# Routing from unscaled rows, zeroing in two parts, and waits between GpSimd's scatters in a gated attention and mixture-of-experts block

## The reference, cut to what matters

```python
# layer 0, attention part: a mixing matrix added to x
x = x + tanh(g_xattn[0]) * L0_xattn(ctx_512, layernorm(x))     # top 76 of 256 per row, sigmoid, symmetrised
# layer 0, feed-forward part: 64 experts, 8 for each token
h = layernorm(x)
logits = h @ gate_w.T                       # (1024, 64)
probs = softmax(logits); topk_w, topk_idx = top_k(probs, 8)
# for each expert e:  out += combine[:, e] * (silu(h @ w13_g.T) * (h @ w13_u.T)) @ w2.T
x = x + tanh(g_ffn[0]) * out
# layer 1: causal attention of 16 heads, and 8 experts plus a shared one
```

## Time and profile before

| | |
|---|---|
| median of 3 runs | 559.7 us (559.28 to 561.05) |
| the profiled execution, its time | 562.27 us |
| the profiled execution, its span in the trace | 560.5 us |
| PE busy | 415.2 us (74%) |
| DVE busy | 342.2 us (61%) |
| ACT busy | 184.9 us (33%) |
| POOL busy | 145.7 us (26%) |
| DMA moved | 82.96 MB |

### The profile page before, as it was taken

One profiled execution on the slowest core, in us unless ns is written; L12 is line 12 of the kernel. 1 busy time (PEld: TensorE's weight loads), 2 busy tenths in 40 slices (PEclk: granted clock), 3 DMA queues, 4 the chain that ended last, 5 costly groups with the idle time before them and its releaser, 6 DMA issues.

```text
span 560.5 us, 9184 instructions
## 1 busy us (share of the span) xinstructions
PE 415.2 (74%) x2710; PEld 351.7 (63%) x2710; DVE 342.2 (61%) x1058; ACT 184.9 (33%) x377; POOL 145.7 (26%) x156
## 2 busy tenths in 40 slices
PE   5344644200999999999616776899789988998796
PEld 3223433200998888998414554787679867996695
DVE  4999793300497448544356784388657885680664
ACT  3122220200333333343271153425363354417321
POOL 4017677575000000000768332411423000000000
PEclk9966565555899999999755679799889999999999
DMA  7999222144999999999422211110111000000000
GB/s 236 427 414 399 83 99 102 61 159 146 278 339 334 325 311 306 350 398 393 142 81 82 60 39 39 47 30 12 58 47 56 2 0 0 20 2 2 2 19 20
DMA packets 36789, 82.96 MB, mean 148 GB/s; under 512 B 6032, under 2 KB 16144, under 8 KB 34960
## 3 DMA queue, kind: packets, MB, share of 16 engines
q1 hardware_dynamic: 23616, 56.48, 29.0%
q0 software_dynamic: 6144, 16.79, 9.2%
q10 hardware_dynamic: 6992, 9.24, 4.6%
HBM read 50.44 MB, written 31.92 MB: 147 GB/s over the span
## 4 chain that ended last, share of the span: by engine, by line
PE 51%; issue 23%; SPq 9%; DVE 7%; ACT 6%; DMA 2%; DVEq 0%; ACTq 0%
PE PS L624 10%; PE PS L634 6%; PE PS L713 5%; PE PS L790 3%; SPq L347 3%; PE PS L687 3%; PE PS L611 3%; PE PS L726 3%; PE PS L728 3%; PE PS L727 3%; PE PS L808 2%; PE PS L775 2%; DMA XE<-slots_in 2%; PE PS L818 2%; SPq L343 2%
## 5 line engine op out<-in xcount | busy, mean ns | idle before, releaser
L467 POOL DMA_INDIRECT GB<-slots_out,IDXG x64 | 69.4, 1084 | 226.5 <-DMA slots_out<-OE 132.3
L624 PE MATMUL PS<-XTE,WR 128*128 128x128 f32 (+2 forms) x512 | 79.6, 299 | 0.0
L460 POOL DMA_INDIRECT slots_in<-XNA,IDX x64 | 62.9, 982 | 33.2 <-issue 18.2
L624 PEld LDWEIGHTS PS<-XTE,WR 128*128 128x128 f32 x512 | 70.3, 193 | 0.4 <-ACT XTE L936 0.2
L1369 DVE TENSOR_TENSOR HE<-SGE,PS 128x128 f32<-128x128 f32 (+2 forms) x64 | 19.9, 311 | 70.1 <-ACT SGE L945 67.2
L634 PE MATMUL PS<-WR,HE 128*80 128x256 f32 (+2 forms) x198 | 53.4, 380 | 0.4 <-issue 0.4
L726 PE MATMUL PS<-XH,WGH 128*128 128x256 f32 x160 | 51.2, 320 | 0.0
L936 ACT COPY XTE<-PS 128x256 f32<-128x256 f32 (+2 forms) x64 | 26.3, 411 | 71.2 <-PE PS L611 71.2
L611 PE MATMUL PS<-CF,XE 80*128 80x80 f32 (+2 forms) x198 | 28.3, 256 | 26.5 <-DMA XE<-slots_in 26.5
L713 PE MATMUL PS<-WD,XW 128*128 128x256 f32 x160 | 42.6, 390 | 5.8 <-DVE TH L1460 5.8
L728 PE MATMUL PS<-XH,WGL 128*128 128x256 f32 x160 | 46.5, 290 | 0.0
(11 more groups left out here) (235 smaller groups left out, 822.2 us busy)
## 6 DMA issues: line engine op xcount, KB each, us to landing
WR<-in_wexp SPq DMA_DIRECT2D x64, 384.0 KB, 5.6
slots_in<-GB SPq DMA_DIRECT2D x12, 1024.0 KB, 19.0
XE<-slots_in SPq DMA_DIRECT2D x24, 160.0 KB, 4.8
slots_out<-OE ACTq DMA_DIRECT2D x24, 160.0 KB
XE<-slots_in SPq DMA_DIRECT2D x29, 128.0 KB, 5.4
slots_out<-OE ACTq DMA_DIRECT2D x24, 128.0 KB
WGU<-in_wgu SPq DMA_DIRECT2D x1, 2560.0 KB
XE<-slots_in SPq DMA_DIRECT2D x11, 192.0 KB, 4.0
```

What stands on the lines that cost most here:

```text
L460: pool.indirect_dma_start(out=xs, out_offset=bass.IndirectOffsetOnAxis(ap=IDX[:, t, j:j + 1], axis=0), in_=XNA[:, t, :], in_offset=None, b ...
L467: pool.indirect_dma_start(out=GB[:, t % BT, j, :], out_offset=None, in_=ys[0:rows, :], in_offset=bass.IndirectOffsetOnAxis(ap=IDXG[:, t, j ...
L624: last = mm(psGE[place % 2][:, a, 0:cap(place)], W13[:, k, a, :], XTE[:, place % 2, k, 0:cap(place)], start=(k == 0), stop=(k == KC - 1))
```

## The change

Five things are different. POOL's `norm_scale` writes to a tile RSN with a column pair for every token tile, so the scale of a batch stays. The gate is made mean-free once (`centre_gate`: PE multiplies the gate by a matrix of -1/256, DVE adds the result), and PE transposes the unscaled rows X1, so that the logits come out as the normalised ones without the factor 1/sqrt(var + eps); the exponential applies this factor (`scale=RSN`), and the emergency path transposes XNA for itself. ACT does the exponential of batch `b` behind `scores(b + 2)` and `base(b + 2)`. Zeroing is in two parts: slots 0 to 127 of every expert (8 DMAs), then slots 128 to 191 (4 DMAs); the first tile's scatters wait for the first part alone. POOL waits, ahead of scatters 10, 11, 13 and 15 of each batch, for the next batch's `summed`, `xn_flipped`, `logits_done` and `ranked`, and `norm_scale` stands ahead of scatter 11 in all batches. DVE's steps stand after other numbers of rounds.

```diff
-ROOT_BEHIND = (None, 10, 7, 7)
+PACE = {10: "summed", 11: "xn_flipped", 13: "logits_done", 15: "ranked"}
+LOW = 128
...
-FIRST_ROUNDS = (1, 3, 5, 6)
-LATER_ROUNDS = (3, 5, 8, 9)
+FIRST_ROUNDS = (1, 2, 2, 3)
+LATER_ROUNDS = (3, 4, 4, 5)
...
             sp.wait_ge(S["zero_set"], 1)
-            for i in range(SLOTS // (8 * P)):
-                sp.dma_start(xs[i * 8 * P:(i + 1) * 8 * P, :].rearrange("(p r) d -> p (r d)", p=P), ZERO)\
-                  .then_inc(S["zeroed"], 16)
+            by_expert = xs.rearrange("(e c) d -> e c d", c=CAP)
+            for e in range(0, E0, 8):
+                part = by_expert[e:e + 8, 0:LOW, :].rearrange("e (q r) d -> q e (r d)", q=16)
+                sp.dma_start(part, ZERO).then_inc(S["zeroed_low"], 16)
+            for e in range(0, E0, 16):
+                part = by_expert[e:e + 16, LOW:, :].rearrange("(x y) (q r) d -> q x y (r d)", y=2, q=16)
+                sp.dma_start(part, ZERO.rearrange("p (y f) -> p y f", y=2)).then_inc(S["zeroed"], 16)
...
+            nc.gpsimd.memset(MINUS_MEAN[:, :], -1.0 / D).then_inc(S["half_set"], 1)
...
-            pool.wait_ge(S["zeroed"], 16 * (SLOTS // (8 * P)))
+            pool.wait_ge(S["zeroed_low"], 16 * (E0 * LOW // (8 * P)))
             for t in range(TT):
+                if t == 1:
+                    pool.wait_ge(S["zeroed"], 16 * (E0 * (CAP - LOW) // (8 * P)))
                 pool.wait_ge(S["xn_ready"], t // BT + 1)
                 pool.wait_ge(S["idx_ready"], t // BT + 1)
                 for j in range(TOP0):
                     b = t // BT + 1
-                    if b < B and t % BT * TOP0 + j == ROOT_BEHIND[b]:
+                    nth = t % BT * TOP0 + j
+                    if b < B and nth in PACE:
+                        pool.wait_ge(S[PACE[nth]], b + 1)
+                    if b < B and nth == 11:
                         norm_scale(b)
...
+            def centre_gate():
+                pe.wait_ge(S["half_set"], 3)
+                for k in range(KC):
+                    last = mm(psN, MINUS_MEAN[:, :], GATE0[:, k, :], start=(k == 0), stop=(k == KC - 1))
+                last.then_inc(S["gate_summed"], 1)
+
             def logits(b):
-                pe.wait_ge(S["xn_ready"], b + 1)
+                pe.wait_ge(S["x1_kept"], b + 1)
                 pe.wait_ge(S["xnt_copied"], b)
                 for k in range(KC):
                     for t in range(BT):
-                        last = nc.tensor.transpose(psX[:, k, t * P:(t + 1) * P], XNA[:, b * BT + t, k * P:(k + 1) * P], ident)
+                        last = nc.tensor.transpose(psX[:, k, t * P:(t + 1) * P], X1[:, b * BT + t, k * P:(k + 1) * P], ident)
...
+                if b == 0:
+                    pe.wait_ge(S["gate_centred"], 1)
...
-                act.wait_ge(S["mask_ready"], b + 1)
-                for t in range(BT):
-                    n = b * BT + t
-                    last = A.activation(C0[:, n, :], psL[:, t, :], ACT.Exp, bias=SM[:, n, 0:1], accum_out=SM[:, n, 1:2])
-                last.then_inc(S["exp_done"], 1)
                 if b + 2 < B:
                     scores(b + 2)
                     base(b + 2)
+                act.wait_ge(S["bias_ready"], b + 1)
+                act.wait_ge(S["rs_ready"], b + 1)
+                for t in range(BT):
+                    n = b * BT + t
+                    last = A.activation(C0[:, n, :], psL[:, t, :], ACT.Exp, scale=RSN[:, n, 0:1], bias=SM[:, n, 0:1], accum_out=SM[:, n, 1:2])
+                last.then_inc(S["exp_done"], 1)
...
-                st.done(V.tensor_scalar(SM[:, b * BT:(b + 1) * BT, 0:1], L8[:, :, 0:1], -1.0, None, ALU.mult))
...
                 V.tensor_tensor(MB[:, b * BT:(b + 1) * BT, :], psL, LR[:, :, :], ALU.not_equal).then_inc(S["mask_ready"], 1)
+                V.scalar_tensor_tensor(SM[:, b * BT:(b + 1) * BT, 0:1], L8[:, :, 0:1], -1.0, RSN[:, b * BT:(b + 1) * BT, 0:1],
+                                       ALU.mult, ALU.mult).then_inc(S["bias_ready"], 1)
+
+            def centre_gate():
+                dve.wait_ge(S["gate_summed"], 1)
+                for k in range(KC):
+                    last = V.tensor_tensor(GATE0[:, k, :], GATE0[:, k, :], psN, ALU.add)
+                last.then_inc(S["gate_centred"], 1)
...
             top_rounds(0, 0, 6)
             base_scale(0, slice(0, BT))
+            centre_gate()
             top_rounds(0, 6, ROUNDS)
```

More of the change, by code:

```diff
@@ L191, in gated_block @@
         LR = sb("LR", [P, BT, E0])
+        RSN = sb("RSN", [P, TT, 2])
+        MINUS_MEAN = sb("MINUS_MEAN", [P, P])
         MB = sb("MB", [P, TT, E0], BF16)
@@ L272, in gated_block @@
             projected qk_copied scores_done sim_copied th_ready masked summed xn_ready xn_flipped
-            xnt_copied logits_done max_ready exp_done dve_scalar dve_mix act_mix x1_kept
+            xnt_copied logits_done exp_done dve_scalar dve_mix act_mix x1_kept
             stats_ready rs_ready coef_ready base_ready var_ready rsx_ready half_set eps_added
             gu_done silu_done h_done o_done o_used
-            zero_set zeroed mask_ready masks_added ranked idx_ready scattered order_set order_done order_ready flag_ready w8_ready
+            zero_set zeroed_low zeroed gate_summed gate_centred bias_ready mask_ready masks_added ranked idx_ready scattered order_set order_done order_ready flag_ready
             all_stored general_done gb_used xt_flipped xt_copied gue_done silue_done he_done oe_done oe_copied dve_w8
@@ L425, in _ @@
             nc.gpsimd.memset(MINUS_HALF[:, :], -0.5).then_inc(S["half_set"], 1)
+            nc.gpsimd.memset(MINUS_MEAN[:, :], -1.0 / D).then_inc(S["half_set"], 1)
             nc.gpsimd.memset(GB[:, 1, 6:, :], 0.0).then_inc(S["half_set"], 1)
-            pool.wait_ge(S["half_set"], 2)
+            pool.wait_ge(S["half_set"], 3)
             def row_scale(part, tiles):
@@ L445, in norm_scale @@
                 pool.wait_ge(S["var_ready"], b + 1)
-                nc.gpsimd.tensor_scalar(RS[:, :, 3:4], MV[:, :, 1:2], EPS, None, ALU.add).then_inc(S["eps_added"], 1)
+                tiles = slice(b * BT, (b + 1) * BT)
+                nc.gpsimd.tensor_scalar(RSN[:, tiles, 1:2], MV[:, :, 1:2], EPS, None, ALU.add).then_inc(S["eps_added"], 1)
                 pool.wait_ge(S["eps_added"], b + 3)
-                nc.gpsimd.tensor_tensor(RS[:, :, 0:1], RS[:, :, 3:4], MINUS_HALF[:, 0:BT].unsqueeze(2), ALU.pow).then_inc(S["rs_ready"], 1)
+                nc.gpsimd.tensor_tensor(RSN[:, tiles, 0:1], RSN[:, tiles, 1:2], MINUS_HALF[:, 0:BT].unsqueeze(2), ALU.pow).then_inc(S["rs_ready"], 1)
             row_scale(1, slice(BT, TT))
             norm_scale(0)
-            pool.wait_ge(S["zeroed"], 16 * (SLOTS // (8 * P)))
+            pool.wait_ge(S["zeroed_low"], 16 * (E0 * LOW // (8 * P)))
             for t in range(TT):
+                if t == 1:
+                    pool.wait_ge(S["zeroed"], 16 * (E0 * (CAP - LOW) // (8 * P)))
                 pool.wait_ge(S["xn_ready"], t // BT + 1)
@@ L649, in all_tokens @@
             def all_tokens():
+                for b in range(B):
+                    pe.wait_ge(S["xnt_copied"], B + b)
+                    for k in range(KC):
+                        for t in range(BT):
+                            last = nc.tensor.transpose(psX[:, k, t * P:(t + 1) * P], XNA[:, b * BT + t, k * P:(k + 1) * P], ident)
+                    last.then_inc(S["xn_flipped"], 1)
+                pe.wait_ge(S["xnt_copied"], 2 * B)
                 with pe.Fori(0, E0 // 2) as i:
@@ L963, in all_tokens @@
                         act.wait_ge(gathered[t][j], 16)
+                for b in range(B):
+                    act.wait_ge(S["xn_flipped"], B + b + 1)
+                    A.copy(XNT[:, :, b * N:(b + 1) * N], psX).then_inc(S["xnt_copied"], 1)
                 with act.Fori(0, E0) as e:
@@ L1180, in mix_norm @@
                 for t in range(BT):
-                    last = V.tensor_scalar(XNA[:, b * BT + t, :], X1[:, b * BT + t, :], MV[:, t, 0:1], RS[:, t, 0:1], ALU.subtract, ALU.mult)
+                    last = V.tensor_scalar(XNA[:, b * BT + t, :], X1[:, b * BT + t, :], MV[:, t, 0:1], RSN[:, b * BT + t, 0:1], ALU.subtract, ALU.mult)
                     if t < BT - 1:
```

## The result

Over 18 runs of each, the changed kernel's median is 556.16 us (551.88 to 558.48) against 559.74 (558.07 to 563.2). The ratio is 0.9941 with a 95% interval of 0.9924 to 0.9958: 3.3 us faster by the ratio (2.4 to 4.3), 3.6 by the medians. The forecast was 9.7, that is 550.0 with an own range up to 552.5; the direction and the path were right, the size was not.

A forecast was written before the change was run, and what follows sets the result against it. POOL's scatter queue was taken to bound the routing stage. Start 6.1 plus waits 5.7 less 0.4 rounding gave 11.4, less 1.7 for late signals 9.7: 559.7 to 550.0 us, own range 547.5 to 552.5, full range 546.5 to 556.5.

The forecast's parts named there:

- the pricing of the late signals: Routing stage, batch 3: engines starting late although their awaited work is done cost 0 to 5.5 us; 1.7 taken.
- clean sum: Routing stage: start 6.1 earlier, waits 5.7 less, minus 0.4 rounding; 11.4 us saved, last scatter ending at 123.6.
- POOL's queue sets the end of the stage and a microsecond off it is one off the time: Routing stage ends with POOL's last scatter, 134.98 before; each microsecond taken from it should come off the time.
- Zeroing in two parts, patterns at full rate: Ahead of the scatters: new patterns cost nothing, low part lands near 32.7, second part is hidden at 43 to 44.
- Mean-free gate, chain of batch 0: Batch 0: two additions cost DVE 0.4 us; slot numbers and first scatter come at 37.0 instead of 43.08.
- Batches 1 to 3 with signals on time: Routing's later batches: POOL waits 1.3 us for batch 1, none for 2 and 3; last scatter ends at 123.6.
- The wait of 4.7 in batch 3 goes: Batch 3: POOL no longer waits for the statistics at scatter 11, where before it lost 4.7 us.
- Rival 1: Batches 2 and 3: late signals return in full, new waits hand them to POOL; saving 5, 554.7 us; chance 0.22.
- Rival 3: Zeroing pattern runs at half rate, low part lands at 54, no scatter before it; 563 us; chance 0.03.
- rival 2: Batches 0 to 2: twelve new waits expose POOL to late signals, costing 14 against 11.4; 562.5 us; chance 0.07.
- Rival 4: Early scatters queue behind second-layer weight loads, the start's 6.1 is lost; 554 to 555 us; chance 0.05.
- the case of no gain: A stage behind the routing gives the saving back; 559.7 us; chance 0.03.

The follow-up runs named there:

- group 2: Kernel before, changed kernel and two variants without the pacing waits, beside the kernel before at 559.15; changed kernel 556.89 us, ratio 0.9947.
- x3: Kernel before with only the two-part zeroing DMAs and their two waits; 551.97 us, ratio 0.9989 to the kernel before.
- x1_no_pace: Changed kernel without the four waits ahead of scatters 10, 11, 13 and 15; 546.79 us, ratio 0.9887 to the kernel before.
- a1_fourth: Changed kernel, nothing altered, run a fourth time beside the kernel before; 549.55 us, ratio 0.9897.
- group 4: Changed kernel and variants without pacing waits, with no rows moved or scatters held, beside the kernel before at 560.08; changed kernel 556.03 us, ratio 0.9917.
- x1_again: Changed kernel without the four pacing waits, run a second time; 556.33 us, ratio 0.995 to the kernel before.
- x8_again: Changed kernel without the pacing waits, scatters issued but no rows moved, run a second time; 555.61 us.
- x4_third: Changed kernel without pacing waits, scales computed ahead, all scatters held until batch 3's slot numbers are there, third run; 607.77 us.
- x6: Changed kernel without pacing waits, norm_scale ahead of scatter 14, DVE's norm behind place for batches 1 to 3; 563.9 us, ratio 1.0073.

## Why the prediction was right or wrong

The step that failed is the pricing of the late signals. The clean sum (11.4) took away a wait of 4.7 that the order doesn't demand, and the term for late signals in the new kernel was put at 1.7. Measured where signals are late, the changed kernel's last scatter ends 7.2 behind the clean sum (130.82 for 123.6): 11.4 less 7.2 is the 4.2 of the traces. In detail:

- *POOL's queue sets the end of the stage and a microsecond off it is one off the time*: right. On chips with late signals the end moves by 4.2 (first traces) and 3.5 (group 2: 134.51 to 130.97); by the medians the time moves by 3.6 and 2.3, by the ratio of group 2 by 3.0 (1.0 to 4.9).
- *Zeroing in two parts, patterns at full rate*: right. The eight DMAs of the low part were issued by 16.2 and landed within 15.8 each, so by about 32 (32.7); the second part is hidden; x3 shows no cost. The first scatter is at 38.02 (37.0): the slot numbers came at 36.94 as forecast, POOL 1.1 behind them. That part of the step I had not counted, so the start gave 5.1 and not 6.1.
- *Mean-free gate, chain of batch 0*: right, numbers at 36.94 for 37.0.
- *Batches 1 to 3 with signals on time*: right to 0.5 us (copy to X1 of batch 3 at 91.65 for 92.1, last scatter's end at 123.86 for 123.6), shown by x1_no_pace and a1_fourth. That the end fits to 0.3 is partly luck: in that trace the start is 0.7 later than forecast (37.75 for 37.0) and the waits cost 0.4 less (0.9 for 1.3).
- *The wait of 4.7 in batch 3 goes*: this half of the step failed. It was booked as a gain from the order. Had the copy not been late, the statistics of batch 3 would have been there when POOL came; x3's trace has no such wait. So 4.7 of the 11.4 were a late signal in the kernel before, and the sum compared a before with it to an after that had 1.7 for all of them. Where signals are on time there is no wait to remove: the old order ends at 129.17 (x3), the changed kernel at 123.86, 5.3 apart, and the ratio 0.9897 of 553.8 is 5.7 us. (The kernel before itself has no trace with signals on time; x3 stands for it, with a start 0.5 to 0.8 earlier.) Where they are late, the wait does go, but they come back elsewhere.
- *Price of the late signals, 1.7 out of 0 to 5.5*: the other half, mis-sized, and outside its bounds. Between a chip with late signals and one without, the changed kernel's end moves by 7.0 (130.82 to 123.86), and by 8.0 to the trace of group 4 (131.82). I gave the one unknown only to batch 3; the trace after has it in the chains of batches 2 and 3, and also behind DVE's own instructions, which pushed mask(3) from the forecast 87.3 to 91.73.
- Rival 1 (late signals come back, 554.7 against 556.16 measured) was the case that happened; it was given 0.22. It deserved more, since the earlier trace rows showed three late starts in one execution and nothing in the change removes their cause. One part of it is wrong: the new waits aren't what hands the lateness to POOL, as x1 ends no earlier without them. Rival 3 is refuted by the start at 38.02 and by x3. In rival 2 POOL did stand at the waits (0.9, 1.4 and 2.1), but without them, in x1, the same time is spent on the statistics and the slot numbers instead. Rival 4 and the case of no gain didn't happen.

## What to carry to other kernels

A wait in a trace has two parts: what the order demands, and how late the signal came behind the work it waited for. Before a removed wait is booked as a gain, work out whether it would exist with the signal on time; if not, it is lateness that the new kernel can meet as well, at any place. A sum of exact steps is worth no more than the one term that was read from a single execution; a second trace on another chip costs little; here it would have shown this one on three chips of five.

## What the runs showed of the hardware

- Signals between engines, and from an engine to itself, were late by 1 to 6 us on some chips while POOL issued indirect DMAs back to back (4.8 from PE to ACT in the kernel before, 5.9 from PE to DVE in x1_again, 1.7 behind DVE itself in x8_again). On others, running the same program, ACT's copies to X1 start within 0.04 us of mix's end. The kernel before takes 559.7, 559.15 and 560.08 where a trace shows late signals, 554.12, 555.07 (one run) and 553.8 where none does; the difference of some 5 to 6 is about that between the ends of their last scatters, 134.98 and, in x3, 129.17.
- They need POOL's scatters (x4_third, one trace) and not the rows that these move (x8_again, one trace). Several were delivered when POOL stopped: 1.7 us behind its last scatter in the changed kernel (104.37 to 106.04), 1.5 in x6, 2.9 in the kernel before.
- SP's three weight DMAs went out within 13.44 and 12.03 us in the two traces of the kernel before, and within 2.6 where signals were on time, but also within 2.64 in the changed kernel with late signals; what decides this stays open.
